# Filler products on TensorE in the ends of both layers of a two-layer latent-attention kernel

## The reference

```python
eq = jax.nn.elu(q); ek = jax.nn.elu(k)
qn = eq / norm(eq); kn = ek / norm(ek)
kv = einsum('bhsd,bhse->bhde', kn, v)
ctx = einsum('bhsd,bhde->bhse', qn, kv) / sqrt(HD)
attn_out = _layernorm(ctx @ Wo + bo + x, g1, be1)
out = _layernorm(_gelu(attn_out @ W1 + b1) @ W2 + b2 + attn_out, g2, be2)
```

## Time and profile before

| | before |
|---|---|
| median of 3 runs | 1162.07 us |
| the 3 runs | 1161.97, 1162.07, 1167.69 us |
| profiled execution, its own time | 1160.7 us |
| its span (first to last instruction) | 1158.9 us |
| TensorE busy | 1114.2 us, 96% |
| VectorE, ScalarE busy | 660.4, 662.8 us, 57% each |
| mean clock granted to TensorE | 0.994 of full speed |

### The profile page before, as it was taken

The page is one execution under the profiler, slowest core; times in us unless marked ns, Lnnn a source line. Parts: engine busy times, 40 slices in busy tenths (PEclk is TensorE's granted clock), DMA queues, the critical chain, the costliest instruction groups (busy, mean ns, idle before and its releaser), DMA issues.

```text
span 1158.9 us, 28671 instructions
## 1 busy us (share of the span) xinstructions
PE 1114.2 (96%) x10008; PEld 926.7 (80%) x10008; DVE 660.4 (57%) x1128; ACT 662.8 (57%) x1097; POOL 222.0 (19%) x316
## 2 busy tenths in 40 slices
PE   6999799999999999999987999999999999999998
PEld 4888688888888888888863888888887888888874
DVE  4999654444444444444464788888886344444443
ACT  1898343343433433433231688888888989999420
POOL 0000100000000000000003677777760220000310
PEclk9999999999999999999999999999999999999999
DMA  3454611000101011001445576767666896665370
GB/s 131 136 140 132 266 66 35 29 27 27 36 27 27 27 36 27 27 28 36 196 137 209 176 234 226 231 225 229 217 233 206 297 319 210 203 197 186 143 301 6
DMA packets 63578, 163.42 MB, mean 141 GB/s; under 512 B 6912, under 2 KB 8384, under 8 KB 58368
## 3 DMA queue, kind: packets, MB, share of 16 engines
q1 hardware_dynamic: 54592, 119.06, 32.0%
q0 software_dynamic: 8960, 44.00, 9.9%
HBM read 124.21 MB, written 38.80 MB: 141 GB/s over the span
## 4 chain that ended last, share of the span: by engine, by line
PE 88%; DVE 6%; DMA 3%; issue 1%; ACT 1%; POOL 0%; DVEq 0%; SPq 0%; ACTq 0%; POOLq 0%
PE ps L687 61%; PE ps L937 8%; PE ps L871 7%; PE ps L722 2%; PE ps L675 1%; DMA q_le<-k_mem 1%; PE ps L733 1%; PE ps L737 1%; PE ps L734 1%; PE ps L735 1%; PE ps L736 1%; PE ps L1088 1%; DMA wx<-xq_in 1%; DMA wa<-ex_in 1%; PE ps L1249 1%
## 5 line engine op out<-in xcount | busy, mean ns | idle before, releaser
L1465 DVE TENSOR_TENSOR wide<-wide,probs 128x1024 f32<-128x1024 f32 x97 | 118.9, 1225 | 226.3 <-ACT probs L536 225.9
L1395 DVE TENSOR_TENSOR wide<-ps,wide 128x512 f32<-128x512 f32 (+1 forms) x194 | 185.2, 954 | 28.4 <-PE ps L687 23.8
L521 ACT CAST wide<-ps 128x512 bf16<-128x512 f32 x294 | 162.3, 586 | 31.6 <-PE ps L687 26.6
L536 ACT ACTIVATE probs<-ps 128x512 f32<-128x512 f32 x196 | 114.7, 599 | 79.8 <-PE ps L687 79.8
L687 PE MATMUL ps<-q_ha,t_ha 128*128 128x512 f32 x392 | 156.3, 399 | 3.8 <-DVE q_le L1325 3.8
L546 ACT ACTIVATE probs<-ps 128x1024 f32<-128x1024 f32 x132 | 128.1, 1027 | 17.9 <-PE ps L687 15.9
L1403 DVE TENSOR_TENSOR wide<-wide 128x512 bf16<-128x512 bf16 (+1 forms) x194 | 107.5, 554 | 11.5 <-ACT wide L521 1.1
L687 PE MATMUL ps<-q_ab,q_hk 128*128 128x512 f32 x392 | 107.5, 394 | 1.4 <-DVE q_ab L1331 1.3
L687 PEld LDWEIGHTS ps<-q_ha,t_ha 128*128 128x128 f32 x392 | 74.9, 191 | 21.5 <-DVE q_le L1325 4.2
L531 ACT COPY weights_q<-ps 128x512 f32<-128x512 f32 x48 | 28.2, 587 | 106.0 <-PE ps L871 90.0
L1453 DVE COPY v_sb<-wide 128x256 f32<-128x256 f32 x98 | 28.7, 295 | 103.8 <-PE ps L937 103.2
(11 more groups left out here) (400 smaller groups left out, 2415.0 us busy)
## 6 DMA issues: line engine op xcount, KB each, us to landing
raw<-ctx_in SPq DMA_DIRECT2D x147, 256.0 KB, 2.7
k_mem<-q_hk SPq DMA_DIRECT2D x49, 512.0 KB, 3.0
v_mem<-probs SPq DMA_DIRECT2D x49, 256.0 KB, 3.4
wide<-v_mem SPq DMA_DIRECT2D x49, 256.0 KB, 4.0
q_le<-k_mem SPq DMA_DIRECT2D x17, 512.0 KB, 4.4
q_ab<-k_mem SPq DMA_DIRECT2D x16, 512.0 KB, 4.0
q_hk<-k_mem SPq DMA_DIRECT2D x16, 512.0 KB, 4.1
ring<-ex_in POOLq DMA_DIRECT2D x5, 1152.0 KB, 13.3
```

The lines of the kernel that those rows point to most:

```text
L521: act.copy(half16[:, c:c + 512], ps[:, back_bank(layer, q) + u, :]).then_inc(sem(f"half{layer}"), 1)
L536: act.activation(e_keep[GT * slot + j][:, u * 512:(u + 1) * 512], ps[:, s_bank[j][u], :], ACT.Exp).then_inc(sem("exp0"), 1)
L1395: dve.tensor_tensor(r, scores, r, ALU.max).then_inc(sem(f"front{layer}"), 1)
L1465: dve.tensor_tensor(run[:, 0:1024], run[:, 0:1024], e, ALU.add).then_inc(sem("lsum"), 1)
```

## The change

All fillers are removed that stand behind the first layer's last value product, in both ends: the 161 products listed below. Kept are those of `turn_x(0)` (2), those within `cross` (4 and 4 in layer 0, 8 and 12 in layer 1) and those of `turn_x(3)` (8 and 2), which stands at the head of layer 1's cross-attention. Waits, products, their order and all other engines are as they were.

```diff
             def turn_x(n, k, src, fill=10, bank=3):
-                keep_warm(fill, bank)
+                keep_warm(fill if n in (0, 3) else 0, bank)
                 pe.wait_ge(sem("xn"), n + 1)
...
-                keep_warm(2, bank)
+                keep_warm(2 if n in (0, 3) else 0, bank)
                 pe.wait_ge(sem("xt"), k + 1)
...
-            keep_warm(2, 7)
             pe.wait_ge(sem("den"), 1)
...
-            keep_warm(2, 7)
             for b in range(4):
                 pe.wait_ge(sem("ot"), b + 1)
...
-            keep_warm(14)
             pe.wait_ge(sem("q_a"), 1)
...
-            keep_warm(5, 7)
             for c in range(4):
                 pe.wait_ge(sem("prob_a"), c + 1)
...
             def project(n, src, w, at):
-                keep_warm(4)
                 pe.wait_ge(sem("head_out"), n + 1)
...
-                keep_warm(2)
                 pe.wait_ge(sem("head_t"), n + 1)
...
-            keep_warm(26)
             pe.wait_ge(sem("unit_qk"), 1)
...
-            keep_warm(4, 7)
             pe.wait_ge(sem("kv"), 1)
...
-            keep_warm(2, 7)
             pe.wait_ge(sem("lin"), 1)
...
-            keep_warm(8)
             pe.wait_ge(sem("ff_hid"), 1)
...
-            keep_warm(4, 5)
             pe.wait_ge(sem("scores_r"), 1)
...
-            keep_warm(14, 5)
             pe.wait_ge(sem("picked"), 1)
...
-            keep_warm(1, 5)
             pe.wait_ge(sem("taken"), 1)
...
-            keep_warm(4, 5)
...
-            keep_warm(3, 6)
             pe.wait_ge(sem("tokens"), 3)
```

## The result

The changed kernel takes 1175.53 us (median of 4 runs, 1175.05 to 1177.17) against 1162.02 for the kernel before (median of 4): ratio 1.0115, with an interval of 1.0094 to 1.0136. So it is 1.2% slower. The profiled execution has a span of 1173.2 us, 14.3 more than before, and the mean granted clock is 0.965 in place of 0.994.

The account below looks back on a forecast made before the run. TensorE, busy 96% of the span and almost always at 2.4 GHz, was taken as the bound. The profiled 1160.7 + 1.2 (layer 0's end) + 0.5 (restart behind the load) + 11.6 (layer 1's end) gave 1174.0 us, range 1166 to 1181.

Parts of the forecast that it names:

- The rest: Outside layer 1's end: layer 0's end +1.2 us, and the restart behind the last experts' load +0.5.
- The gain of the overruns: Layer 0's end: fillers outlasting their waits delay scores and the probabilities' transposes; removing them gains 2.2 us.
- The q, k, v: Layer 0: clock falls in the idle gap before them, +1.7 us (0 to 2.5); layer 1: half-clocked throughout, +2.5.
- The rank's delay: Layer 0: half-clocked shared-expert records lose about 2 us, of which 0.8 reaches the chain through the rank behind them.
- The gathering's own restart: Layer 0: gathering and first `up0` follow another 2 to 3 us gap; half a chance of a restart, 0.9 us taken.
- `kv` to projection: Layer 1's end: `kv`, `lin` and the projection, 12 records, run at low clock once 52 filler records go: +1.9 us.
- `up`: Layer 1's feed-forward, 32 records: first dense work, so a clock restart, +2.4 us (1.7 to 3.4).
- `down`: Layer 1's feed-forward, behind a 2.2 us gap while ScalarE makes the gelu: +0.5 us (0 to 1.7).
- `up1`: Layer 1's end, 64 records with nothing dense before them: a restart at their head, +2.5 us (1.7 to 3.5).
- That the clock holds through gaps under 3 us: Rival: clock falls only at `unit_qk` and behind L1190; 1165.6 us, 1168 with middling restarts; chance 0.17.
- Restarts at the lowest price: Rival for both ends: the clock returns at the first chance each time, 1170.6 us; chance 0.2.
- That the ends keep the clock by themselves: Rival: sparse products hold the clock in both ends, leaving only the overruns' gain; 1158.3 us, chance 0.05.

Follow-up runs that it names:

- the experiment: From the kernel before, fillers removed in layer 1's end alone: 1.0100, 11.6 us slower; where 1.9 is quoted, in layer 0's end alone: 1.0016.
- the thin fillers: Kernel before with both ends' fillers using 16 rows of the array in place of 128, and half as many: ratio 1.0153, 17.8 us slower.
- the trimmed kernel: Kernel before with layer 0's overruns removed: 14 fillers ahead of the scores become 9, 5 ahead of the probabilities' transposes 0, two pairs one each; ratio 0.9983.
- the first experiment: Kernel before with the fillers of layer 0's end alone removed: ratio 1.0016, 1.9 us slower.
- the kernel whose clock hardly falls, the last kernel: The trimmed kernel with fillers added in gaps where the clock fell, layer 1's end exactly as before: ratio 0.9938, 1154.74 us.

## Why the prediction was right, point by point

**The sum.** Forecast 1174.0 with 1166 to 1181, measured 1175.53. Layer 1's end was forecast at +11.6: the profiles have +12.0, the experiment 11.6. The rest was forecast at +1.7; the profiles have 3.2 + 0.9 + 0.5 = +4.6 behind the start, the experiment 1.9. The terms make 13.3 us and the runs 13.5; the forecast lies 1.5 below the measured time because the terms were put on 1160.7, one execution, and not on the median. That the sums come so close is partly luck, as the terms below show.

**The clock as the cause** is shown by the same records taking up to twice as long where the granted clock reads 0.50, and by the thin fillers: as many as in the kernel with half the fillers, in the same places, and 12.7 us slower, some of it overruns.

**The gain of the overruns**, forecast at 2.2 us for layer 0, is shown at 1.7 in the trimmed kernel's profile from q, k, v on and at 2.0 (0.5 to 3.5) by its runs. In the changed kernel it cannot be seen by itself, as the low clock covers it.

**Terms of layer 0 that came out otherwise.** The q, k, v cost 5.35 - 2.92 = 2.4 us, near the upper bound of 2.5, where I took 1.7. The scores fell into a second low stretch (580 to 583) that my sum did not have: from the first part to the fourth they took 5.0 us, before 3.3. `turn_x(1)`, `turn_x(2)` and the router, which had no term, cost 0.9 together. The rank's delay, 0.8, did not come: TensorE's timeline, after, reads

```profile
597.29 4.25 PE L687 MATMUL ps<-xt,ring 128*128 128x128 f32 x24
601.38 0.29 PE L1056 MATMUL ps<-sm,cst 128*128 128x16 f32 x2
603.89 1.98 PE L687 MATMUL ps<-probs,xn 128*128 128x512 f32 x4 [2.22 <-DVE probs L1612]
```

The 24 records lost 1.3 and not 2, the clock came back while they ran, and from their start to the gathering it is 6.60 us, before 6.61. By the starts of the same instructions the 3.2 us of layer 0's end are 0.9 for those transposes and the router, 1.4 from q, k, v to the scores (the 2.4 lost, 1.0 of overrun regained) and 1.0 from the scores to the turning of the attention's output, less 0.1 ahead of them. The last values came 1.0 us later behind the scores' start, where even without the full clock I had them 0.5 earlier. The gathering's own restart (0.9, half a chance) is absent here and present in the first experiment: a coin, as it was put.

**Terms of layer 1.** Forecast and measured, from the earlier trace rows and the chain above: q, k, v 2.5 and 1.8; `kv` to projection 1.9 and 2.2 (0.71 + 0.23 + 0.73 + 1.15 before became 1.22 + 0.44 + 1.23 + 2.09); `up` 2.4 and 2.3; `down` 0.5 and 1.6 (5.35 for 3.72); the gathering 0.9 and 1.0; `up1` 2.5 and 0.9. L1190 stayed hidden, as said; it even ran at the full clock (3.69 us in both). The transposes cost 0.5 and not 0.8, the router and the choice of tokens 1.1 and not 0.3. One piece was forgotten: the product of `project(1)`, four records, went from 1.15 to 2.09, +0.9. So the sum is right to half a us and its terms are not. The q, k, v were taken as half-clocked to their end, but the clock came back between 1098 and 1099, inside them. `up1` was priced as a restart from nothing, 9 to 10.5 us; it took 7.87, as the clock came back 1.6 us after its start, behind the gathering and two transposes. Those errors, 0.7 and 1.6, pay for most of `down`, `project(1)` and the choice.

**A reading to correct.** The 8.58 us of the earlier trace rows, behind which the clock fell at 625, is the load's time on the chain. TensorE still worked during the first part of it and stood idle for 4.80 us. No term used the 8.58.

**The rivals.** That the clock holds through gaps under 3 us is excluded: it was low in 570 to 575, behind a gap of 2.7 us. Restarts at the lowest price (1170.6, or 1171.9 if put on the median) lie below the interval, which is 1172.9 to 1177.8 us. `down` (1.6), which that rival had at nothing, the forgotten `project(1)` and the q, k, v of layer 0 (2.4 for 1.7) cost more than that; `up1` (0.9 for 1.7) cost less. The Trainium skill's figure ("TensorE: Matmul & The Clock Gate", Part 1: the warming up costs under 1% of a typical span) would, by my estimate from it, have put the time below 1172.3 us; the measured 1.15% is above, though its interval reaches down to 0.94%. Against the kernel whose clock hardly falls the changed one loses 1.8%. That the ends keep the clock by themselves is excluded by every profile without fillers.

**What stays open.** Why the clock falls in one gap and not in another of the same length was not settled: identical code in layer 0's end took 39.4 us in two profiles (before, and fillers removed in layer 1 alone) and 40.9 in two others. Why half the fillers held the clock in some gaps only is part of the same question. Only 16 and 128 rows were tried, nothing between. Which of the five added fillers of the last kernel carry its gain was not tried one by one.

## What to carry to other kernels

In a chain of small products that wait on other engines, fillers that end just before the wait does are worth their place: taking them out cost 1.2%, and most of it (9.4 of 13.4 us) in the part where a gap of 6 us stood ahead of a run of short products. Look first for gaps without fillers and for fillers that run past their wait, both read from the chain of waits; mending those two gave 0.6%. Fillers of 128 rows did the work and fillers of 16 rows did not; and in a gap where the clock may already be low, a filler lasts twice as long. Before crediting an edit with 1 or 2 us of a profile, compare the stretch in several profiles of unedited code.

## What the runs showed of the hardware that was not expected

Products of 16 rows keep TensorE busy and not its clock: in the kernel before it was never idle from 1116 to 1128, and the clock fell at 1123 behind L1190; 164 filler records of 16 rows left the kernel 12.7 us slower than 164 of 128 rows. Nor is a busy engine with full rows always enough: in the profiles of the trimmed kernel, of the half-filled one and of the two with parts of layer 1's fillers removed, the clock fell near 564 while TensorE was hardly idle, soon after sixteen records of one column. With the same instructions, an execution's clock falls at different places from run to run. That moves the 40 us from L977 to the gathering by 1.5 us, and the stretch from there to layer 1's first key product, with the same code, between 33.4 and 37.0 us; a single profile is no measure of less. At half clock a lone transpose pair took 0.70 us on the changed kernel's chain against 0.45, so short steps lose somewhat less than dense work, which doubles.
